# Half words turned by DMAs, scores in four full banks, a new VectorE order, and copies of the state's diagonal blocks

## The chip, the cores and the metric

One core of a Trainium2 chip runs the whole program in one launch. The metric is the device time in microseconds (us), the median over several runs. TensorE (PE) multiplies matrices, VectorE (DVE), ScalarE (ACT) and GpSimd (POOL) do the rest, SyncE (SP) issues most DMAs.

## The reference

A transformer block on x of shape (2, 2048, 512), float32:

```python
xn  = layernorm(x)                       # no affine part
# linear attention with decay, 16 heads of 32, chunks of 128 tokens
h   = rmsnorm(xn, qkv_norm_w);  q, k, v = h @ ternary(qkv_w).T
scores = einsum('bhtd,bhsd,hts->bhts', q, k, mask)        # within a chunk
o   = scale * (scores @ v + (q * lam_t) @ S)              # S: state, 32 x 32 per head
S   = lam_T * S + (k * lam_rev).T @ v
att = rmsnorm(rmsnorm(o, norm_w), proj_norm_w) @ ternary(proj_w).T
# feed-forward: 8 routed experts (top 2), width 256, and a shared expert, width 1024
router = softmax(xn @ w_gate)
ffn = sum over the two chosen e of c_e * (silu(xn @ g_e) * (xn @ u_e)) @ d_e  +  shared(xn)
out = x + att + ffn
```

## The kernel before

Products that need more than float16 are done with two half words: a high one, the float16 of a value, and a low one, the float16 of what is left. A product of two split values takes three passes of float16 matmuls (high by high, high by low, low by high); the ternary weights are exact in float16, so q, k, v and the projection take two passes.

The program runs in blocks, with all engines meeting between them: the setup of the weights; `attention` (16 steps); `shared(0)`, the shared expert on the first half of the tokens, beside which VectorE and ScalarE route the tokens and split the experts' weights; `routed()`, 72 tiles of 128 gathered rows; and `shared(1)`, the shared expert on the second half and the final sums.

A step of `attention` takes one chunk of 128 tokens of both sequences (u = 0 and 1). It is software-pipelined: in step n each engine works on the back part of chunk n (scores, outputs, state, norms, projection) and on the front part of chunk n+1 (its q, k, v, router logits), and VectorE already norms chunk n+2. The order of the work is written out by hand, per engine, in the functions `step` of `attention`; each engine goes through its list in order and waits on semaphores. PSUM has a ring of three banks (class `Ring`, which lists what passes through them in which order), a tensor `sc` of four banks for the scores and one bank `o_ps`.

What the change touches in a step:

- `xn_turn` (L624): TensorE transposes the normed tokens of the next chunk, ScalarE copies them out (`take_xnT`, L807), makes the high half words of h (`h_high`, L822, with the norm weight as scale) and of xn (`x_high`, L814); VectorE makes the low ones of h (`h_low`, L972), GpSimd those of xn (`x_low`, L1160).
- `scores` (L671): for each u four sets of four heads, each into two banks of `sc`, of which a set uses half; VectorE scales and masks each set (`decayed_scores`, L1026). The sets of u = 0 of the next chunk stand around v0 in TensorE's list.
- `o_back` (L709) transposes the output of a u back to token order; `o_square`, `o_mean`, `normed` (L853, L1052, L1065) are the first RMS norm, `on_squares`, `second_norm` (L863, L1073 to L1077) the second; GpSimd multiplies by the weight (`weighted`, L1183); TensorE transposes (`o_turn`, L727), ScalarE and VectorE split (`y_high`, L869, `y_low`, L1083), TensorE projects (`proj`, L736), VectorE adds the residual (L1093).
- `outer` makes k^T v for all pairs of heads of a group, `masked_kv` (L1043, VectorE) keeps the diagonal blocks by a multiplication with a 0/1 mask, and GpSimd updates the state (`update`, L1175, L1178); `decayed_q` (L1166) is GpSimd's too.
- VectorE also norms chunk n+2: `row_stats` (L923), `norm_stats` (L930 to L940), `norm` (L945, L949), `norm_factors` (L956 to L964), and takes the maxima of a part of the experts' weights (`weight_maxima`, L988).

xn goes to `xn_dram` in float32 for the gather of the routed tiles, its half words to `xT_dram` for the shared expert. In `routed()` a tile is gathered (L1250, GpSimd), split (L1918, ScalarE; L1850, GpSimd), turned by a DMA transpose that SP issues (L1823), and multiplied (L1280, L1287).

Of the kernel before, what the change touches and what calls it, by code (L numbers as in the profile page):

```python
# [12 lines left out]
P = 128  # L13
# [44 lines left out]
class Ring:  # L58
# [4 lines left out]
    FRONT = ["xnT0", "xnT1", "q0", "q1", "rt", "k0", "k1", "v0", "v1"]  # L63
    STEP = ["xnT0", "xnT1", "kTr0", "ot0", "kv0", "q0", "q1", "kTr1", "ot1", "rt", "onT0", "k0", "kv1", "k1", "proj0",
            "onT1", "v0", "v1", None, None, "proj1"]
    LAST = ["kTr0", "ot0", "kv0", "kTr1", "ot1", "onT0", "kv1", "proj0", "onT1", "proj1"]
# [38 lines left out]
def build(nc, x, qkv_w, qkv_nw, proj_w, proj_nw, norm_w, s, w_gate, w_gu, w_dn, w_sgu, w_sdn, out):  # L105
# [7 lines left out]
    xn_dram = nc.dram_tensor("xn_dram", [B * N, C], F32, kind="Internal").ap()  # L113
    xT_dram = nc.dram_tensor("xT_dram", [NCH, P, KT, 2, B * P], F16, kind="Internal").ap()
# [4 lines left out]
    xn_steps = xn_dram.rearrange("(b n p) c -> n p b c", b=B, p=P)  # L119
# [6 lines left out]
    with ExitStack() as kept:  # L126
# [40 lines left out]
        bmask = sb(attn, "bmask", [P, P])  # L167
        nw_b = sb(attn, "nw_b", [P, DIM])
        pnw_b = sb(attn, "pnw_b", [P, DIM])
        hw = sb(attn, "hw", [P, KT])  # L170
# [13 lines left out]
        with setup_ctx as c:  # L184
# [16 lines left out]
            qnw_c = sb(c, "qnw_c", [P, KT])  # L201
# [49 lines left out]
            SMALL = 16 * (1 + HPT + 5)  # L251

            @block.scalar
            def _(act):
                with nc.allow_non_contiguous_dma(reason="small vectors laid out as columns"):
# [7 lines left out]
                    act.dma_start(qnw_c[:], qkv_nw.rearrange("(k p) -> p k", p=P)).then_inc(in_small, 16)  # L263
# [48 lines left out]
            def _(v):  # L312
# [8 lines left out]
                link(v.memset(bmask[:], 0.0))  # L321
                for h in range(HPT):
                    v.memset(bmask[HD * h:HD * h + HD, HD * h:HD * h + HD], 1.0)
# [49 lines left out]
                v.tensor_scalar(hw[:], qnw_c[:], scales[:, 0:1], 1.0 / X_SCALE, ALU.mult, ALU.mult)  # L373
# [43 lines left out]
def mask_heads():  # L417

    return [HPT * (2 * (s // 2) + gg) + 2 * (s % 2) + jj for s in range(4) for jj in range(2) for gg in range(2)]


def attention(nc, ctx, sb, sem, k):
# [3 lines left out]
    qkvT, projT, wg16, ginv, mask, lamq, lamrev, lamT, bmask = (k[x] for x in "qkvT projT wg16 ginv mask lamq lamrev lamT bmask".split())  # L426
    nw_b, pnw_b, hw, alpha, state = (k[x] for x in "nw_b pnw_b hw alpha state".split())
    ident16, ounit, ounit2, xl, xl_in = (k[x] for x in "ident16 ounit ounit2 xl xl_in".split())
    x_steps, x1_steps, xn_steps, NCH, B = k["x_steps"], k["x1_steps"], k["xn_steps"], k["NCH"], k["B"]
# [10 lines left out]
    with ExitStack() as c:  # L440
# [3 lines left out]
        xnT = sb(c, "xnT", [P, KT, T2])  # L444
        x16 = sb(c, "x16", [P, 2, KT, 2, T2], F16)
        wraw = sb(c, "wraw", [P, 2, START[4]])
        hh = sb(c, "hh", [P, KT, T2], F16)
        hl = sb(c, "hl", [P, KT, T2], F16)
# [4 lines left out]
        probs = sb(c, "probs", [P, B, 4, 4, P])  # L453
# [5 lines left out]
        yh = sb(c, "yh", [P, B, KT, P], F16)  # L459
        yl = sb(c, "yl", [P, B, KT, P], F16)  # L460
# [34 lines left out]
        xn_out = [sem(c, f"xn_out{i}") for i in range(2)]  # L495
        x1_out = [sem(c, f"x1_out{i}") for i in range(2)]
        xT_out = [sem(c, f"xT_out{i}") for i in range(2)]
        wraw_in = [sem(c, f"wraw_in{i}") for i in range(2)]
        names = ("xhigh_ready xlow_ready wmax_ready stats_ready stats_seen mv_ready ve_ready sd_ready rstd_ready xn_ready rve_ready hv_ready hv2_ready hsd_ready "
                 "r_ready r2_ready kscale_ready xnT_ready hh_ready h_ready q_ready k_ready v_ready qlam_ready "  # L500
                 "o_full logits_ready kvm_ready kS_ready ss1_ready z1_ready sq1_ready g1a_ready "
# [22 lines left out]
        def after(q, par):  # L524
            return (q, 1) if par == 0 else (q + 1, 0)

        READ = {"xnT": "xnT_ready", "rt": "logits_ready", "q": "q_ready", "k": "k_ready", "v": "v_ready",
                "kTr": "kS_ready", "kv": "kvm_ready", "ot": "oT_ready", "onT": "yl_ready", "proj": "x1_ready"}
# [23 lines left out]
        def _(sp):  # L552
# [10 lines left out]
            def store_xn(q, par):  # L563
                n = 2 * q + par
                sp.wait_ge(S["xn_ready"], 2 * n + 2)
                sp.dma_start(xn_steps[n] if isinstance(n, int) else xn_steps[bass.ds(n, 1)][0], xn[:, par]
                             ).then_inc(xn_out[par], 16)
# [6 lines left out]
            def store_xT(q, par):  # L574
                n = 2 * q + par
                sp.wait_ge(S["xlow_ready"], n + 1)
                sp.dma_start(xT_dram[n] if isinstance(n, int) else xT_dram[bass.ds(n, 1)][0], x16[:, par]
                             ).then_inc(xT_out[par], 16)

            def prologue():  # L580
                for done_sem in k["setup_sems"]:
                    sp.sem_clear(done_sem)
                store_xn(0, 0)
                load_weights(0, 0)
                store_xT(0, 0)

            def step(q, par, front, norm):
                n = 2 * q + par
                if norm:
                    sp.wait_ge(S["xn_ready"], 2 * n + 2)  # L590
                    load_xl(q + 1, par)
# [3 lines left out]
                sp.wait_ge(S["x1_ready"], 2 * n)  # L595
                load_xr(q, par)
                if front:
                    store_xn(*after(q, par))
                    sp.wait_ge(S["wmax_ready"], n)
                    load_weights(*after(q, par))  # L600
                for u in range(B):
                    if u == 1 and front:
                        store_xT(*after(q, par))
                    sp.wait_ge(S["x1_ready"], 2 * n + u + 1)
                    dst = x1_steps[n] if isinstance(n, int) else x1_steps[bass.ds(n, 1)][0]
                    sp.dma_start(dst[:, u], x1[:, u]).then_inc(x1_out[u], 16)

            run_steps(sp, prologue, step)
            for par in range(2):
# [1393 lines left out]
```

## Time and profile before

| | us |
|---|---|
| median of 3 runs (1401.72 to 1403.88) | 1403.2 |
| the profiled execution's own time | 1401.92 |
| its span, first to last instruction | 1400.2 |
| TensorE busy | 1281.1 |
| VectorE busy | 695.2 |
| GpSimd busy | 527.0 |
| ScalarE busy | 514.0 |

Mean granted TensorE clock: 0.973. An engine's busy time counts from an instruction's start to its end, so pipelined matmuls overlap: two neighbours that take 0.27 us each can start 0.11 us apart. In a timeline the first number is the start, the second the time to the end of the group in that row.

### The profile page before, as it was taken

Reading aid. Unit: us, or ns where it says so; the run is one execution under the profiler, and the core shown is the slowest. Engines: PE = TensorE matmul, PEld = TensorE weight load, DVE = VectorE, ACT = ScalarE, POOL = GpSimd, SP = SyncE. Lnnn points to the kernel's source line nnn. Section 1 sums busy time; section 2 is a strip of 40 time slices with the busy share of each in tenths; the row PEclk is TensorE's granted clock in tenths of the full one; section 3 lists DMA queues with packets and bytes.
Section 4 is the critical chain, followed back from the end, with each engine's and each line's share of the span. In section 5 each row is a group of like instructions: output and inputs, shape, how many; then the busy total and the mean of one; then the engine's idle time right before and its main releaser. Section 6 shows DMA issues by size and latency. Waiting matters only on the chain. (4 is left out here: it accounts for less than half of the span.)

```text
span 1400.2 us, 29499 instructions
## 1 busy us (share of the span) xinstructions
PE 1281.1 (91%) x10418; PEld 879.9 (63%) x10418; DVE 695.2 (50%) x1606; ACT 514.0 (37%) x1034; POOL 527.0 (38%) x467
## 2 busy tenths in 40 slices
PE   1499999999999994999999969999999969999997
PEld 1477777667776673777777734444444447777775
DVE  4477877878878766883333322222222213333323
ACT  3444444444444434432323224544445411111111
POOL 0333344333444332024541035555554542444333
PEclk9699999999999997999999989999999989999999
DMA  5213443334433334524552358888888861443333
GB/s 173 95 60 129 154 145 109 109 131 142 161 109 109 131 125 162 180 93 105 107 138 102 33 136 183 188 194 190 186 191 186 192 190 65 179 164 135 135 136 121
DMA packets 174072, 195.06 MB, mean 139 GB/s; under 512 B 100976, under 2 KB 107248, under 8 KB 174000
## 3 DMA queue, kind: packets, MB, share of 16 engines
q1 hardware_dynamic: 158464, 156.17, 38.0%
q0 software_dynamic: 13328, 37.04, 10.0%
q8 instruction: 55, 0.90, 0.3%
q10 hardware_dynamic: 2208, 0.82, 0.2%
q14 instruction: 17, 0.14, 0.0%
HBM read 117.55 MB, written 56.77 MB: 124 GB/s over the span
## 5 line engine op out<-in xcount | busy, mean ns | idle before, releaser
L1269 PE MATMUL gu<-xT,WG 128*128 128x256 f16 x3072 | 350.3, 275 | 23.5 <-DMA x1s<-x_dram 11.8
L1269 PEld LDWEIGHTS gu<-xT,WG 128*128 128x128 f16 x3072 | 302.7, 99 | 74.8 <-DVE WD L1556 12.4
L1280 PE MATMUL rgu<-WG,raw 128*128 x876 | 215.1, 382 | 14.4 <-issue 10.9
L1695 DVE SCALAR_TENSOR_TENSOR actv<-gu,up_inv,sg 128x512 f32<-128x512 f32 x64 | 48.0, 751 | 252.8 <-ACT sg L1532 252.6
L1532 ACT ACTIVATE sg<-gu,gate_inv 128x512 f32<-128x512 f32 x64 | 43.9, 686 | 319.2 <-PE gu L1269 319.2
L1287 PE MATMUL yp<-WD,ah 128*128 128x512 f16 x512 | 152.3, 379 | 1.0 <-DVE al L1700 1.0
L1280 PEld LDWEIGHTS rgu<-WG,raw 128*128 128x128 f16 x876 | 86.1, 98 | 105.5 <-issue 23.2
L1850 POOL TENSOR_TENSOR xsp<-xg,xsp 128x512 f16<-128x512 f32 x75 | 86.7, 1157 | 105.2 <-ACT xsp L1918 105.2
L655 PE MATMUL ring<-hh,qkvT 128*128 128x256 f16 x512 | 116.4, 276 | 6.0 <-DVE hl L972 6.0
L1250 POOL DMA_INDIRECT xg<-xn_dram,idx x77 | 73.8, 958 | 123.9 <-POOL xsp L1850 66.4
L655 PE MATMUL ring<-hl,qkvT 128*128 128x256 f16 x512 | 116.4, 275 | 0.0
L1765 POOL DMA_INDIRECT raw<-y_dram,gidx x64 | 63.6, 994 | 133.7 <-DVE ys L1676 105.4
L1970 DVE TENSOR_TENSOR alr<-rat,ahr 128x256 f16<-128x256 f32 x72 | 30.5, 424 | 160.0 <-ACT ahr L1938 160.0
L1160 POOL TENSOR_TENSOR x<-xnT,x 128x1024 f16<-128x1024 f32 x16 | 34.3, 2142 | 198.8 <-ACT x L814 198.8
L1749 POOL DMA_INDIRECT slot_dram<-payload,posi x64 | 62.8, 981 | 116.5 <-DVE posi L1645 57.8
L1287 PE MATMUL yp<-WD,al 128*128 128x512 f16 x256 | 97.0, 379 | 0.0
L1026 DVE SCALAR_TENSOR_TENSOR probs<-sc,r,mask 128x512 f32<-128x512 f32 x128 | 89.7, 742 | 3.4 <-PE sc L671 3.4
L1287 PE MATMUL ryp<-WD,ahr 128*128 x288 | 85.9, 379 | 0.0
L1287 PEld LDWEIGHTS yp<-WD,ah 128*128 128x128 f16 x512 | 49.7, 98 | 49.3 <-DVE al L1700 2.5
L1924 ACT ACTIVATE raw<-ryp,out_inv 128x512 f32<-128x512 f32 x72 | 49.5, 687 | 65.9 <-PE ryp L1287 65.9
L1183 POOL TENSOR_TENSOR on<-on,pnw_b 128x512 f32<-128x512 f32 x32 | 40.7, 1273 | 77.1 <-DVE on L1065 77.1
L1700 DVE TENSOR_TENSOR al<-actv,ah 128x512 f16<-128x512 f32 x64 | 46.5, 726 | 44.5 <-ACT ah L1535 44.5
(237 smaller groups left out, 2163.2 us busy)
## 6 DMA issues: line engine op xcount, KB each, us to landing
y_dram<-raw SPq DMA_DIRECT2D x72, 256.0 KB
xl<-in_L_attn_x SPq DMA_DIRECT2D x16, 512.0 KB, 4.5
xn_dram<-xn SPq DMA_DIRECT2D x16, 512.0 KB, 6.4
wraw<-in_L_ffn_w_gate_up SPq DMA_DIRECT2D x16, 512.0 KB, 6.9
xT_dram<-x SPq DMA_DIRECT2D x16, 512.0 KB, 2.8
xr<-in_L_attn_x SPq DMA_DIRECT2D x16, 512.0 KB, 5.9
x_dram<-x SPq DMA_DIRECT2D x32, 256.0 KB, 2.1
xT<-xT_dram SPq DMA_DIRECT2D x16, 512.0 KB, 6.9
```

The costliest lines, as they stand in the source:

```text
L655: ins = pe.matmul(bank[:, g * T2:(g + 1) * T2], qkvT[:, kk, a:a + P], h[:, kk, :], start=(kk == 0 and h is hh), stop=(kk == KT - 1 and h i ...
L1026: v.scalar_tensor_tensor(out=probs[:, u, s].rearrange("p (j g) t -> p j (g t)", j=2), in0=sc[:, 2 * pair:2 * pair + 2, 0:2 * P], scalar=r[ ...
L1250: pool.indirect_dma_start(out=xg[:, par], out_offset=None, in_=xn_dram, in_offset=bass.IndirectOffsetOnAxis(ap=idx[:, par, 0:1], axis=0)). ...
L1269: ins = pe.matmul(gu[:, h, f * tokens:(f + 1) * tokens], w[:, kk, b, a0:a0 + P], x[:, kk, a], start=(kk == 0 and (a, b) == PASSES[0]), sto ...
L1280: ins = pe.matmul(gu[bank][:], x(kk, a), w[:, 0, kk, b, :], start=(i == 0), stop=(i == len(done) - 1))
L1287: ins = pe.matmul(y[:], act_hl[a][:, f, :], w[:, f, b, :] if len(w.shape) == 4 else w[:, 0, f, b, :], start=(first and f == 0 and (a, b) = ...
L1695: v.scalar_tensor_tensor(out=actv[:, g % 2], in0=gu[g % 2][:, 1].rearrange("p (f t) -> p f t", f=FT), scalar=up_inv[:, 1:2], in1=sg[:], op ...
L1700: v.tensor_tensor(al[:, g % 2], actv[:, g % 2], ah[:, g % 2], ALU.subtract).then_inc(S["al_ready"], 1)
L1749: pool.indirect_dma_start(out=slot_dram, out_offset=bass.IndirectOffsetOnAxis(ap=posi[:, kk, t:t + 1], axis=0), in_=payload[:, kk, t, :], ...
L1765: pool.indirect_dma_start(out=gy[:, u, i], out_offset=None, in_=y_dram, in_offset=bass.IndirectOffsetOnAxis(ap=gidx[:, u, i:i + 1], axis=0 ...
L1850: pool.tensor_tensor(xsp[:, par, 1], xg[:, par], xsp[:, par, 0], ALU.subtract).then_inc(S["low_ready"], 1)
L1924: act.activation(ysb[:, par], yp[par][:], ACT.Copy, scale=out_inv[:, 0:1]).then_inc(S["y_ready"], 1)
```

## The change

All transposes of half words become DMA transposes. h and xn are split in token order (`hs`, `xs`), and so is the second norm's output (`ys`); SP turns each [128, 1024] float16 tile into [128, 8, 128]. GpSimd multiplies xn by the norm weight (`weighted_h`). The half words of xn in token order go to `xs_dram`, from where the routed tiles are gathered already split, four tiles deep, so `routed()` has no split any more. The scores of a u fill all four banks and are masked in two operations of 1024 columns. The diagonal blocks are copied by ScalarE, four small copies a u, into a tile that was set to zero once. VectorE's, ScalarE's, GpSimd's and SP's lists are reordered.

```diff
-    STEP = ["xnT0", "xnT1", "kTr0", "ot0", "kv0", "q0", "q1", "kTr1", "ot1", "rt", "onT0", "k0", "kv1", "k1", "proj0",
-            "onT1", "v0", "v1", None, None, "proj1"]
+    STEP = ["kTr0", "ot0", "kv0", "q0", "q1", "kTr1", "ot1", "rt", "k0", "kv1", "k1", "proj0", "v0", "v1", "proj1"]
...
# SP
+            def turn_h(q, par):
+                n = 2 * q + par
+                if not (isinstance(n, int) and n == 0):
+                    wait_apart(sp, S["v_ready"], 2 * n, S["sp_passed"])
+                for u in range(B):
+                    wait_apart(sp, S["hl_ready"], 2 * n + u + 1, S["sp_passed"])
+                    sp.dma_start_transpose(hT[:, u], hs[:, u].rearrange("p a c -> p (a c)")).then_inc(hT_in[u], 16)
...
             def step(q, par, front, norm):
                 n = 2 * q + par
+                if front:
+                    turn_h(*after(q, par))
+                    turn_x(*after(q, par))
...
                 if front:
-                    store_xn(*after(q, par))
                     sp.wait_ge(S["wmax_ready"], n)
                     load_weights(*after(q, par))
+                    store_xs(*after(q, par))
+                    store_xT(*after(q, par))
                 for u in range(B):
+                    turn_y(u, q, par)
+                store_x1(0, q, par)
...
# TensorE
             def step(q, par, front, norm):
-                if front:
-                    xn_turn(0, *nxt, st)
-                    xn_turn(1, *nxt, st)
                 k_turn(0, q, par, st)
-                scores(1, q, par, (0, 1))
+                scores(1, q, par)
                 outputs(0, q, par, st)
-                scores(1, q, par, (2, 3))
...
-                o_turn(0, q, par, st)
...
                 proj(0, q, par, st)
                 if front:
-                    scores(0, *nxt, (0, 1))
-                o_turn(1, q, par, st)
-                if front:
+                    scores(0, *nxt)
                     project("v0", *nxt, st)
-                    scores(0, *nxt, (2, 3))
                     project("v1", *nxt, st)
                 proj(1, q, par, st)
...
# ScalarE
+            def take_kv(u, q, par, st):
...
+                for j in range(HPT):
+                    own = slice(HD * j, HD * j + HD)
+                    ins = act.activation(kvm[own, u, :, own], bank[own].rearrange("p (g e) -> p g e", g=KT)[:, :, own],
+                                         ACT.Copy)
...
                 take_oT(1, q, par, st)
                 o_square(1, q, par)
-                y_high(0, q, par, st)
+                o_root(1, q, par)
+                if norm:
+                    norm_roots(q + 1, par)
                 if front:
                     take("k0", *nxt, st)
-                o_root(1, q, par)
+                on_squares(1, q, par)
+                y_high(1, q, par)
                 if front:
                     take("k1", *nxt, st)
-                on_squares(1, q, par)
+                take_kv(1, q, par, st)
...
# VectorE, the whole new order
                 scaled_k(0, q, par, st)
+                decayed_scores(1, q, par)
                 o_mean(0, q, par)
                 normed(0, q, par)
+                weight_maxima(q, par, (1, 2, 3))
+                scaled_k(1, q, par, st)
+                second_norm(0, q, par)
+                y_low(0, q, par)
                 if has_norm:
                     row_stats(0, q + 1, par)
                     row_stats(1, q + 1, par)
                 if front:
                     take_logits(*nxt, st)
+                if has_norm:
+                    norm_stats(q + 1, par)
                 o_mean(1, q, par)
                 normed(1, q, par)
                 if has_norm:
+                    norm(q + 1, par)
+                    norm_factors(q + 1, par)
                 second_norm(1, q, par)
+                y_low(1, q, par)
                 weight_maxima(q, par, (0,))
+                residual(0, q, par, st)
+                if front:
+                    decayed_scores(0, *nxt)
+                else:
+                    weight_scales()
+                if has_norm:
+                    h_low(q + 1, par)
                 residual(1, q, par, st)
...
# GpSimd
+            def weighted_h(q, par):
+                n = 2 * q + par
+                for u in range(B):
+                    pool.wait_ge(S["xn_ready"], 2 * n + u + 1)
+                    if not (isinstance(n, int) and n == 0):
+                        pool.wait_ge(S["hl_ready"], 2 * n + u - 1)
+                    pool.tensor_tensor(hn[:, u], xn[:, par, u], hw_b[:], ALU.mult).then_inc(S["hn_ready"], 1)
...
                 weighted(1, q, par)
+                if norm:
+                    weighted_h(q + 1, par)
                 update(1, q, par)
...
# experts
-                            ins = pe.matmul(gu[:, h, f * tokens:(f + 1) * tokens],
+                            ins = pe.matmul(gu[:, h, f * tokens:(f + 1) * tokens].rearrange("p (u t) -> p u t", u=B),
                                             w[:, kk, b, a0:a0 + P],
-                                            x[:, kk, a], start=(kk == 0 and (a, b) == PASSES[0]),
+                                            x[:, :, a * KT + kk, :], start=(kk == 0 and (a, b) == PASSES[0]),
...
                 def _(pool):
-                    def low_part(q, par):
...
+                    for r in range(XG, TURNS):
+                        pool.wait_ge(turned[r % XH], 16 * ((r - XG) // XH + 1))
+                        gather(pool, r)
```

## Rows read from the trace of the kernel before

**Rows 1.** Windows, whole attention and one microsecond: length, busy per engine, granted clock, DMA share, GB/s.

```profile
61.00:541.00 480.00, 454.47 (x4978) 343.27 (x4979) 372.67 (x891) 207.52 (x487) 183.01 (x128) 0.99 0.37 127
...
531.00:532.00 1.00, 1.00 (x6) 1.00 (x7) 0.47 (x1) 0.03 (x1) 0.92 (x2) 0.50 1.05 382
```

**Rows 2.** Timeline of TensorE, one step: start, us, engine, line, what, [idle before].

```profile
297.60 0.66 PE L709 MATMUL o_ps<-ident,oT 128*128 128x128 f32 x4
...
304.74 0.74 PE L671 MATMUL sc<-qT,kT 32*128 32x128 f32 x16
305.41 0.66 PE L727 MATMUL ring<-ident,on 128*128 128x128 f32 x4
...
312.14 0.38 PE L736 MATMUL ring<-projT,yh 128*128 128x512 f16 x1 [0.87 <-ACT vS L832]
...
313.87 1.04 PE L624 MATMUL ring<-ident,xn 128*128 128x128 f32 x8
314.88 0.66 PE L679 MATMUL ring<-ident,kT 128*128 128x128 f32 x4
...
327.05 0.66 PE L709 MATMUL o_ps<-ident,oT 128*128 128x128 f32 x4
```

**Rows 3.** Timelines of VectorE and of GpSimd, where both work at once.

```profile
302.52 1.18 DVE L934 TENSOR_SCALAR ve<-mv 128x2 f32<-128x2 f32 x1
...
302.42 1.27 POOL L1183 TENSOR_TENSOR on<-on,pnw_b 128x512 f32<-128x512 f32 x1 [1.68 <-DVE on L1065]
...
57.89 0.48 DVE L972 SCALAR_TENSOR_TENSOR hl<-xnT,hw,hh 128x256 f16<-128x256 f32 x1 [3.55 <-ACT hh L822]
...
59.09 2.34 DVE L972 SCALAR_TENSOR_TENSOR hl<-xnT,hw,hh 128x256 f16<-128x256 f32 x1
...
58.88 2.26 POOL L1160 TENSOR_TENSOR x<-xnT,x 128x1024 f16<-128x1024 f32 x1 [9.35 <-ACT x L814]
...
329.56 0.20 DVE L1052 TENSOR_SCALAR z<-ss,r2m 128x1 f32<-128x1 f32 x1
...
327.87 2.35 POOL L1166 TENSOR_TENSOR qlam<-qT,lamq 128x1024 f32<-128x1024 f32 x1
```

**Rows 4.** Timeline of VectorE, the operations whose place changes.

```profile
309.35 1.00 DVE L949 TENSOR_SCALAR xn<-xl,mv,rstd 128x512 f32<-128x512 f32 x2
...
314.74 0.15 DVE L956 RECIPROCAL r<-hsd 128x2 f32<-128x2 f32 x1
...
315.66 0.69 DVE L1034 TENSOR_TENSOR kS<-ring,kscale 128x512 f32<-128x512 f32 x1
...
322.59 0.20 DVE L1052 TENSOR_SCALAR z<-ss,r2m 128x1 f32<-128x1 f32 x1
...
323.46 0.75 DVE L1065 SCALAR_TENSOR_TENSOR on<-o_ps,g,nw_b 128x512 f32<-128x512 f32 x1
324.12 1.28 DVE L923 BATCH_NORM_STATS2 stats<-xl 128x6 f32<-128x512 f32 x2
...
328.95 0.69 DVE L1083 TENSOR_TENSOR yl<-ring,yh 128x512 f16<-128x512 f32 x1 [1.54 <-ACT yh L869]
```

**Rows 5.** Timeline of ScalarE, one copy out of PSUM.

```profile
303.12 0.60 ACT L842 ACTIVATE kT<-ring 128x512 f32<-128x512 f32 x1 [1.95 <-PE ring L655]
```

**Rows 6.** DMA queues and issues, 90 to 520 us, then 820 to 1125 us.

```profile
q1 hardware_dynamic: 25552, 53.49, 36.2%
...
q1 hardware_dynamic: 86307, 37.24, 54.6%
...
raw<-xsp SPq DMA_TRANSPOSE x73, 3.1
```

**Rows 7.** Timelines of SP and TensorE where routed() starts, and of TensorE late in attention.

```profile
816.58 1.36 SPq L1823 DMA_TRANSPOSE raw<-xsp  x1
...
822.16 6.48 PE L1280 MATMUL rgu<-WG,raw 128*128 x18 [10.89 <-issue]
...
530.82 0.90 PE L709 MATMUL o_ps<-ident,oT 128*128 128x128 f32 x3 [2.99 <-ACT oT L847]
```

More of the change, by code:

```diff
@@ L646, in project @@
                     for kk in range(KT):
-                        for h in (hh, hl):
-                            ins = pe.matmul(bank[:], h[:, kk, i * P:(i + 1) * P], qkvT[:, kk, 2 * DIM:3 * DIM],
-                                            start=(kk == 0 and h is hh), stop=(kk == KT - 1 and h is hl))
+                        for a in range(2):
+                            ins = pe.matmul(bank[:], hT[:, i, a * KT + kk, :], qkvT[:, kk, 2 * DIM:3 * DIM],
+                                            start=(kk == 0 and a == 0), stop=(kk == KT - 1 and a == 1))
@@ L720, in outer @@
                 ins.then_inc(done, 1)
[L722 to L728 removed]
             def proj(u, q, par, st):
                 n = 2 * q + par
[L732 removed]
+                pe.wait_ge(yT_in[u], 16 * (n + 1))
                 bank, done = fill(pe, f"proj{u}", st)
                 for g in range(KT):
[L735 to L737 removed]
+                    for a in range(2):
+                        ins = pe.matmul(bank[:], yT[:, u, a * KT + g, :], projT[:, g, :],
+                                        start=(g == 0 and a == 0), stop=(g == KT - 1 and a == 1))
                 ins.then_inc(done, 1)
             def prologue():
[L741 to L742 removed]
                 for name in ("q0", "q1"):
@@ L946, in norm @@
                 v.wait_ge(S["rstd_ready"], n + 1)
-                v.wait_ge(xn_out[par], 16 * q)
+                if not (isinstance(n, int) and n < 2):
+                    v.wait_ge(S["xlow_ready"], 2 * n - 2)
                 for u in range(B):
@@ L1133, in step @@
                 if has_norm:
-                    norm_stats(q + 1, par)
-                masked_kv(1, q, par, st)
+                    norm(q + 1, par)
+                    norm_factors(q + 1, par)
                 second_norm(1, q, par)
+                y_low(1, q, par)
                 weight_maxima(q, par, (0,))
+                residual(0, q, par, st)
                 if front:
-                    decayed_scores(0, *nxt, (0, 1))
-                residual(0, q, par, st)
-                if has_norm:
-                    norm(q + 1, par)
-                y_low(1, q, par, st)
-                if front:
-                    decayed_scores(0, *nxt, (2, 3))
+                    decayed_scores(0, *nxt)
                 else:
                     weight_scales()
+                if has_norm:
+                    h_low(q + 1, par)
                 residual(1, q, par, st)
-                if has_norm:
-                    norm_factors(q + 1, par)
             run_steps(v, prologue, step)
@@ L1713, in step @@
                                  unit_experts)[i]()
-                            if half == 0 and last and g == 1:
-                                v.wait_ge(slot_in, 16)
-                                index(v, 0, 0)
-                                index(v, 0, 1)
                         if last:
@@ L1799, in routed @@
                 block = c.enter_context(nc.Block())
-                def later(q, par, tiles):
-                    return q + (par + tiles) // 2, (par + tiles) % 2
                 def run_steps(eng, step):
@@ L1855, in _ @@
-                    for r in range(3):
-                        low_part(r // 2, r % 2)
-                    def step(q, par, first):
-                        low_part(*later(q, par, 3))
-                    run_steps(pool, step)
-                    pool.wait_ge(xg_in[0], 16 * (SLOT_TILES // 2 + 3))
-                    pool.wait_ge(xg_in[1], 16 * (SLOT_TILES // 2 + 2))
+                    for r in range(XG, TURNS):
+                        pool.wait_ge(turned[r % XH], 16 * ((r - XG) // XH + 1))
+                        gather(pool, r)
@@ L1904, in some @@
                         for i in range(UNROLL):
-                            tile(UNROLL // 2 * h + i // 2, i, first and i == 0, places)
+                            tile(h, i, first and i == 0, places)
                     some(0, True)
```

395 lines of the change are left out of this document (166 added, 229 removed).

## The prediction

> **What bounds the kernel now.** The page comes first: TensorE is busy for 1281 of the span's 1400 us, and its line in the 40 slices is at 9 nearly everywhere. The windows say the same of the 16 steps of attention: 454 of 480 us, clock 0.99, VectorE 373, DMA 0.37 [rows 1]. The routed tiles are TensorE-bound too. So the stage to read is attention, and the view is the timeline of one step. From one o_back(1) to the next it is 327.05 - 297.60 = 29.45 us [rows 2]. TensorE stands still in it only for about 2 us: 0.87 before proj1, the rest around the split scores and in semaphores. The last step has no front part, so 15 such periods count.
>
> **What leaves TensorE.** Eight transposes of xn (313.87 to 314.88, 1.0 us) and two times four of the second norm (305.41 starts one) at half that, 0.5 each: 2.0 us. The wait before proj1 (0.87) goes, since the onT bank and the ring's two blanks go. If nothing else became late, a period would be 29.45 - 2.0 - 0.9 = 26.6 us, and 15 of them 43 us less. The question is which chain then ends last.
>
> **The chain that I see: from o_back(1) to the scores of the next chunk.** Let x be the start of o_back(1). TensorE has this to do until scores(0): before 304.74 - 297.60 = 7.1 us, without o_turn 6.6. But scores(0) needs k1 copied out, and ScalarE now copies k1 after on_squares(1) and y_high(1), thus after the root of VectorE's second_norm(1); before, k1 stood ahead of on_squares(1). And VectorE now puts norm and norm_factors of chunk n+2 between normed(1) and second_norm(1). Step by step:
> - z(1), the mean of the first norm: before at x + 2.5 (329.56), just behind y_low(0) at 328.95. y_low(0) comes 2.7 us earlier, having lost its transposes and copy (my estimate from GpSimd's product and one copy of 0.60, [rows 3, 5]). Between the two now stand row_stats (1.28, [rows 4]), the logits (0.2) and norm_stats, some 0.6 of small operations and the 1.18 of `ve` [rows 3]: 3.2 us. z(1) is at x + 3.0.
> - from z to the end of `on`: 322.59 to 323.46 + 0.75, 1.62 us [rows 4]. Call the end T = x + 4.6.
> - T starts on3(1) on GpSimd (1.27 us), and right behind it come the two new weighted_h, of the same form as on3 (1.27 each).
>
> Here a behaviour of the rows decides. Where VectorE and GpSimd work at once, VectorE's operations on SBUF alone stand still: `ve`, two elements, took 1.18 us beside GpSimd's product of 302.42 and ended with it; an hl of 57.89 took 0.48 alone, that of 59.09 took 2.34 beside GpSimd's x_low of 58.88. That last pair also shows the order: GpSimd got in between two operations of VectorE that followed each other without a gap. An operation on one element did not stand still (z at 329.56, 0.20, beside decayed_q) [rows 3]. The operations of norm and norm_factors (xn; r2, rv, rc, r2m, kscale) are of the kind that did, and before they all ran while GpSimd was idle. Now:
> - xn waits for on3(1), to T + 1.35; its two operations take 1.0 [rows 4]: T + 2.35.
> - weighted_h of u = 0 takes 1.27: r2 waits to T + 3.6 and ends at 3.8.
> - weighted_h of u = 1 gets in, 1.27: T + 5.05. The rest of the factors, about 0.7 of the 0.92 from 314.74 to 315.66 [rows 4]: T + 5.75.
> - z2 0.2, root 0.2, y_high 0.5 and k1's copy 0.6 (a copy: [rows 5]), 0.1 to TensorE: T + 7.4 = x + 12.0.
>
> So TensorE, done at x + 6.6, stands still for 5.4 us in this stretch. From scores(0) to the next o_back(1) it has work: two times 0.67 for the scores (304.74 to 305.41), v0, v1 and proj1 at 1.73 each (eight matmuls of 512 columns, 312.14 to 313.87), and from k_turn 314.88 to 327.05 12.2 us, where nothing changes [rows 2]: 1.3 + 5.2 + 12.2 = 18.7. The period is 12.0 + 18.7 = 30.7 us, 1.25 more than before, and 15 of them +19 us.
>
> Of xn the trace has no row beside a busy GpSimd. For it speaks its speed: 512 columns in 0.5 us, where bn_stats on as many takes 0.64 (half of 1.28) [rows 4]. The Trainium skill (SBUF — State Buffer, "Who interferes with whom") says that copies, casts and tensor_scalar can enter modes that need the port pair shared with GpSimd, so that one of the two engines stands still for a whole instruction. By that xn is held, as summed here; were only operations with two SBUF operands held, xn would be free and the stretch shorter by 1.1 us a step.
>
> **What else changes, and what hides it.**
> - VectorE: four masks of 512 columns for a u become two of 1024, about 0.6 us less in a step, and masked_kv's two 0.69 go. Neither lies in the stretch above. Zero; had they counted, at most 2 us a step.
> - ScalarE: eight small block copies, bounds 0.15 and 0.6 each (a one-column operation and a full copy [rows 5]), beside TensorE's work; I take 0.3. The copies for v0 and the kv banks come later than k1's but before their banks are asked for.
> - Turned h: SP issues two turns once v1 is copied; issue 1.36 [rows 7], landing 3.1 [rows 6], so hT is there 5 us after v1; q0 starts over 7 us after it. Hidden, with 2 us to spare. SP's loads and stores of a step stand behind these turns, and turn_y behind all of them.
> - Turned y0: y_low(0) ends near x, the turn lands at x + 3.2 on an empty queue and proj0 is due at x + 4.9. Loads, xs and xT are still being moved then, up to 3 us: TensorE may wait 1.4 us before proj0. In my sum that lies within the 5.4 us; without them it would show. Turned y1 is issued about 1 us before scores(0); proj1 comes 4.8 us after it: hidden.
> - DMA work: 53.49 MB took 36.2% of 430 us, 0.76 us for 256 KB. In the routed stretch 54.6% of 305 us, less 73 stores at 0.76, over 73 turns gives 1.5 us a turn, twice a copy of that size [rows 6]. A step goes from 10.7 (0.362 x 29.45) to 19.8 us: under the period.
>
> The Trainium skill (Advanced Engine Details and Errata, "X-Bar Transpose (TRN2)") has transposing DMAs as fast as plain ones; the rows say twice the time. By the page a step would hold 15.3 us of DMA work instead of 19.8; the sum is the same by both.
> - Shared expert: its matmuls (and q's, k's) read the moving operand as two pieces of 128 columns instead of 256 in a row. No row shows such a read. Bounds: 0, and 10% of the 0.11 us between two such matmuls, some 45 us over 4096 of them. I take 0: the routed stage's and the projection's matmuls of 512 columns and these of 256 all run at one pace a column.
> - routed(): bound by TensorE, so the split that goes gives nothing a tile. At its start the first turn was issued at 816.58, behind the split, and TensorE began at 822.16 [rows 7]; now the rows are there already: -1 to -3, I take -2.
> - Ends of attention: proj1 of the last step gets 2 us later, under the scales' chain (weight_scales), which stays ahead of the last residual. Zero, bounds -1 and +3.
>
> **Sum.** 1401.9 (the profiled execution's own time) + 19 - 2 = 1419; the runs' median is 1.3 above it: 1420.
>
> **Rivals.**
> - The port is no matter for these operations (faster). Then T to k1 is xn 1.1, factors 0.9, z2, root, y_high, k1 and 0.1: 3.8 us; scores(0) at x + 8.4, the period 27.1, 15 x -2.35 = -35: 1366. For it: no row has xn held. Against: `ve` and hl.
> - VectorE keeps the port once it has it, so weighted_h of u = 1 doesn't get in: 1.27 less a step, 29.4: about 1400. The pair at 59 us speaks against.
> - The clock falls too (slower still). Late in attention TensorE stood still for 2.99 us before 530.82, three transposes then took 0.90, and the window 531 to 532 was granted 0.50 [rows 1, 7], the level of 1.2 GHz. My sum has a gap of up to 5.4 us in each step, perhaps cut in two by proj0. Three microseconds at half pace cost 1.5: a period of 32.2, +41 - 2, 1442. For it the two gaps near 3 us that the trace has, both with that end; against, that TensorE is busy over 80% around the gap, which it was not there.
> - Turns slower than 1.5 us when four stand in one queue, or the two-piece reads cost: +15 to +45, over 1430. This decides from 2 us a turn (22.7 us of DMA work and all of turn_y behind it).
> - The change does what it says and nothing is late: 1360.
>
> **Chances.** Forecast 0.36; the clock with it 0.20; VectorE keeps the port 0.12; no matter of ports, or nothing late, 0.24; turns or reads 0.08. Range 1362 to 1443; the forecast's own is 1406 to 1432. Within 0.2% (2.8 us) is what a measurement can't tell from no change: 0.08. Faster 0.36, slower 0.56.
>
> **What would show it.** After: xn (L949's successor) near 1.7 us in its first operation, one of r2, rv near 1.4 in each step; ScalarE's root of z2(1) with the longest wait, on VectorE; scores(0) waiting for k1's copy by 3 to 5 us; period 30.7. Wrong if xn keeps its 0.54 us in all steps (27.1), or if TensorE's longest wait is for DMAs (yT, hT). A granted clock under 0.95 in attention is the third rival. The routed tiles should keep 4.1 us, and the shared expert its matmuls' 0.11.

## The result, and the profile after

The changed kernel takes 1438.4 us in the median of 4 runs (1431.9 to 1444.1), the kernel before 1402.5 beside it: a ratio of 1.0255, 95% interval 1.0203 to 1.0307. It is slower by 36 us. The forecast was 1420, slower by 18; the time lies at the rival in which the clock falls too, 1442. The profiled execution took 1441.9 us, with a span of 1440.1 us and a mean granted clock of 0.951 (before: span 1400.2, 0.973).

Windows of the changed kernel over attention and over single microseconds of one step (length, busy time per engine with instructions, granted clock, DMA share, GB/s):

```profile
60.00:590.00 530.00, 460.34 (x4736) 340.31 (x4736) 373.45 (x758) 215.96 (x568) 231.72 (x173) 0.91 0.62 165
...
299.00:300.00 1.00, 1.00 (x14) 1.00 (x17) 1.00 (x1) 0.95 (x4) 0.21 (x1) 0.53 0.00 0
304.00:305.00 1.00, 1.00 (x3) 0.30 (x2) 0.43 (x1) 0.00 (x0) 0.00 (x0) 0.50 0.00 0
306.00:307.00 1.00, 1.00 (x7) 0.41 (x6) 0.00 (x0) 0.07 (x1) 0.00 (x0) 1.00 0.00 0
332.00:333.00 1.00, 0.84 (x18) 0.87 (x22) 1.00 (x2) 0.96 (x5) 0.00 (x0) 1.00 0.00 0
333.00:334.00 1.00, 1.00 (x22) 1.00 (x17) 1.00 (x2) 0.97 (x3) 0.87 (x1) 0.59 0.42 84
336.00:337.00 1.00, 1.00 (x5) 0.44 (x4) 1.00 (x3) 0.00 (x0) 0.00 (x0) 0.70 0.00 0
```

Against [rows 1], TensorE is busy for 87% of the stretch instead of 95%, and the mean granted clock is 0.91 instead of 0.99. The single windows say how: in each step the clock drops to 0.50, the 1.2 GHz level, for a stretch, and comes back. In one step the stretch runs from 299 to about 306 us, in the next from 333 to 337, and so on in turn: 6.8 and 3.4 us, if twice what each window lacks of 1.00 is added up.

TensorE's timeline of that step (start, us, line, what, idle time before and its releaser):

```profile
298.82 2.92 PE L695 MATMUL sc<-qT,kT 32*128 32x128 f32 x32 [2.16 <-issue]
...
321.35 0.66 PE L731 MATMUL o_ps<-ident,oT 128*128 128x128 f32 x4
...
327.94 1.90 PE L750 MATMUL ring<-projT,yT 128*128 128x512 f16 x8 [1.55 <-DMA yT<-ys]
332.16 2.25 PE L695 MATMUL sc<-qT,kT 32*128 32x128 f32 x32 [2.32 <-issue]
```

o_back(1) starts at 321.35 and scores(0) at 332.16, 10.8 us later, where TensorE has 6.9 us of work (6.6 forecast). It stands still twice: 1.55 us before proj0, for the turn of y(0), and 2.32 us before scores(0). In [rows 2] the step's largest gap is 0.87. Behind the wait it works at half pace: the 32 matmuls of the scores take 2.92 and 2.25 us, where they take 1.72 at full clock.

The two engines that the prediction's chain runs through, VectorE first, then ScalarE and GpSimd:

```profile
324.23 0.20 DVE L1050 TENSOR_SCALAR z<-ss,r2m 128x1 f32<-128x1 f32 x1
...
325.15 0.75 DVE L1063 SCALAR_TENSOR_TENSOR on<-o_ps,g,nw_b 128x512 f32<-128x512 f32 x1
...
326.10 1.89 DVE L957 TENSOR_SCALAR xn<-xl,mv,rstd 128x512 f32<-128x512 f32 x2
327.91 0.15 DVE L964 RECIPROCAL r<-hsd 128x2 f32<-128x2 f32 x1
328.10 1.03 DVE L966 TENSOR_TENSOR r<-r 128x2 f32<-128x2 f32 x1
329.05 0.16 DVE L967 TENSOR_SCALAR rv<-r 128x2 f32<-128x2 f32 x1
329.12 1.24 DVE L968 TENSOR_SCALAR rc<-r,ounit 128x2 f32<-128x2 f32 x1
...
330.68 0.14 DVE L1071 TENSOR_SCALAR z<-ss 128x1 f32<-128x1 f32 x1
```

```profile
330.86 0.20 ACT L872 ACTIVATE sq<-z 128x1 f32<-128x1 f32 x1 [4.20 <-DVE z L1071]
330.96 0.61 ACT L878 ACTIVATE ys<-on 128x512 f16<-128x512 f32 x1
331.48 0.58 ACT L838 ACTIVATE kT<-ring 128x512 f32<-128x512 f32 x1
...
325.98 1.26 POOL L1183 TENSOR_TENSOR on<-on,pnw_b 128x512 f32<-128x512 f32 x1 [2.28 <-DVE on L1063]
...
327.69 2.65 POOL L1161 TENSOR_TENSOR raw<-xn,hw_b 128x512 f32<-128x512 f32 x2 [0.44 <-DVE xn L957]
```

T, the end of `on`, is 325.9. xn's pair takes 1.89 us beside on3(1), which ends at 327.24; in [rows 4] it takes 1.00. r2 and rc, two elements in each partition, take 1.03 and 1.24 us beside the two products of weighted_h. ScalarE, having nothing that it may do, waits 4.20 us for z2(1), and k1's copy, which scores(0) wait for, ends at 332.06. So the chain is the one forecast, step by step.

Where the 39.9 us between the two spans are, by the starts of `on`: up to the first one -2.0; 15 periods 484.26 us instead of 440.26, +44.0; the last step +0.1; all behind attention -2.2. A period is 32.28 us in the mean, in turn about 33.3 and 31.7.

### The profile page after: what moved, and what is told of

The parts are those of the page before. It is cut to its first block and busy times, and to the rows that moved or that the text cites. A ratio compares the mean times of both kernels' runs of the same rounds, so it can differ in the third digit from the quotient of the medians.

```text
span 1440.1 us, 27983 instructions
## 1 busy us (share of the span) xinstructions
PE 1282.9 (89%) x10162; PEld 875.7 (61%) x10162; DVE 693.5 (48%) x1396; ACT 482.6 (34%) x1039; POOL 486.5 (34%) x437
## 5 line engine op out<-in xcount | busy, mean ns | idle before, releaser
L1248 POOL DMA_INDIRECT raw<-xs_dram,slots x73 | 69.4, 951 | 299.6 <-DMA raw<-raw 241.3
L680 PE MATMUL ring<-hT,qkvT 128*128 128x256 f16 x1024 | 122.3, 276 | 19.8 <-DMA hT<-hs 18.4
L680 PEld LDWEIGHTS ring<-hT,qkvT 128*128 128x128 f16 x1024 | 101.3, 99 | 32.7 <-issue 20.2
L695 PE MATMUL sc<-qT,kT 32*128 32x128 f32 x1024 | 68.1, 327 | 28.9 <-issue 28.9
L750 PE MATMUL ring<-projT,yT 128*128 128x512 f16 x256 | 67.3, 411 | 29.0 <-DMA yT<-ys 29.0
L695 PEld LDWEIGHTS sc<-qT,kT 32*128 32x128 f32 x1024 | 61.0, 224 | 39.8 <-issue 39.8
L1031 DVE SCALAR_TENSOR_TENSOR probs<-sc,r,mask 128x1024 f32<-128x1024 f32 x64 | 79.1, 1278 | 11.7 <-PE sc L695 11.7
L673 PE MATMUL ring<-qkvT,hT 128*128 128x512 f16 x256 | 76.0, 463 | 0.0
```

Of the source, the lines that this page charges most:

```text
L673: ins = pe.matmul(bank[:], hT[:, i, a * KT + kk, :], qkvT[:, kk, 2 * DIM:3 * DIM], start=(kk == 0 and a == 0), stop=(kk == KT - 1 and a == 1))
L680: ins = pe.matmul(bank[:, g * T2:(g + 1) * T2].rearrange("p (u t) -> p u t", u=B), qkvT[:, kk, w0:w0 + P], hT[:, :, a * KT + kk, :], start ...
L695: ins = pe.matmul(sc[:, j, g * P:(g + 1) * P], kT[rows, par, g, u * P:(u + 1) * P], qT[rows, par, g, u * P:(u + 1) * P], start=True, stop= ...
L750: ins = pe.matmul(bank[:], yT[:, u, a * KT + g, :], projT[:, g, :], start=(g == 0 and a == 0), stop=(g == KT - 1 and a == 1))
L1031: v.scalar_tensor_tensor(out=probs[:, u, pair].rearrange("p j g t -> p j (g t)"), in0=sc[:, 2 * pair:2 * pair + 2], scalar=r[:, par, u:u + 1],
L1248: pool.indirect_dma_start(out=xg[:, r % XG], out_offset=None, in_=xs_dram, in_offset=bass.IndirectOffsetOnAxis(ap=slots[:, r, 0:1], axis=0 ...
```

## The experiments

All times are medians in us; the ratio is to the kernel before, run in the same job (1401.5, 1402.4 and 1399.2). All edits are to the changed kernel. "Steady" is said of the steps from about the fifth on.

**Unneeded matmuls in both gaps.** TensorE gets something to do ahead of the waits for k1 and for y(0), which stay as they are; only the waits for free banks come ahead of the added matmuls, which write there.

```diff
+                    for pair in range(2):
+                        pe.wait_ge(sc_free[pair], 2 * n + u)
+                    for i in range(9):
+                        pe.matmul(sc[:, i % 4, :], hT[:, 0, 0, :], qkvT[:, 0, 0:DIM], start=True, stop=True)
...
+                bank, done = fill(pe, f"proj{u}", st)
+                if u == 0:
+                    for _ in range(6):
+                        pe.matmul(bank[:], hT[:, 0, 0, :], qkvT[:, 0, 0:DIM], start=True, stop=True)
                 pe.wait_ge(yT_in[u], 16 * (n + 1))
-                bank, done = fill(pe, f"proj{u}", st)
```

> TensorE gets work that nobody needs while it would stand still: 6 matmuls of 512 columns ahead of the wait for y0, 9 ahead of the wait for k1 (1.3 and 1.9 us at full pace, against gaps of 1.6 and 2.2 us). Theory (the clock falls over the gaps, on top of the waits): granted clock in attention 0.98 instead of 0.91, period 30.0 to 30.9 us instead of 32.3, total 1438 - 15 x 1.8 = 1411, 1403 to 1420. Rival (the chain through VectorE sets the period, the half pace is absorbed by later waits): no change, 1433 to 1443. Rival (more TensorE work only costs): slower, 1450.

1408.8 (1407.7 to 1411.7), ratio 1.0050 [1.0033, 1.0066]; mean clock 0.979. More work makes it 30 us faster. ScalarE's wait for z2(1) is what it was (61.7 us in 28 times, the longest 4.2, in the changed kernel), so the chain is untouched. The window over attention shows the clock, and TensorE's timeline what changed (waits: engine, line, for whom, sum, times, longest):

```profile
ACT sq L879 <- DVE z L1078: 62.3, 30, 4.2
```

```profile
90.00:540.00 450.00, 435.30 (x4611) 319.46 (x4612) 350.20 (x710) 199.18 (x525) 216.22 (x161) 1.00 0.67 183
```

```profile
314.49 1.89 PE L757 MATMUL ring<-projT,yT 128*128 128x512 f16 x8
316.22 2.11 PE L691 MATMUL sc<-qkvT,hT 128*128 128x512 f16 x9
319.15 1.72 PE L699 MATMUL sc<-qT,kT 32*128 32x128 f32 x32 [0.83 <-issue]
```

The steady period is 30.1 us each time, with no stretch at half pace. So a period's 33.3 and 31.7 split: 30.1 is the late chain, 3.2 and 1.6 the clock, about half of the 6.8 and 3.4 us. By the medians some 29 of the 36 us are the clock's (1438.4 less 1408.8), though the fillers may cost a little themselves. In the two traced executions, 30.1 us apart, 26.4 of them lie before the last `on` of attention. What stands behind it, with the same code in both, takes 863.1 and 859.3 us; in the ten traces of the changed kernel and its variants it takes 852 to 866, so a few us between two totals need not come from attention.

**GpSimd forms h's product last.** weighted_h goes behind update(1), so VectorE's factors meet a quiet GpSimd.

```diff
-                if norm:
-                    weighted_h(q + 1, par)
                 update(1, q, par)
+                if norm:
+                    weighted_h(q + 1, par)
```

> GpSimd does its two products by h's norm weight after update(1) instead of before it. Theory (they hold VectorE's factors, so the root of z2 and k1's copy are late): r2 and rc take 0.16 and 0.22 again, xn stays at 1.9 for two, k1 is out 1.9 us earlier, the gap before scores(0) goes from 2.2 to under 0.5, the clock stays up, period 28.7 to 29.8, total 1385 to 1402. Rival (waits for the turned y0, DMA): that gap stays at 1.6 and the period at 31 or more, over 1420.

1397.4 (1388.4 to 1404.4, 10 runs), ratio 0.9978 [0.9954, 1.0002]. The factors that were held are free, and only they: xn stays beside on3(1).

```profile
307.72 1.89 DVE L957 TENSOR_SCALAR xn<-xl,mv,rstd 128x512 f32<-128x512 f32 x2
...
309.71 0.16 DVE L966 TENSOR_TENSOR r<-r 128x2 f32<-128x2 f32 x1
...
309.86 0.22 DVE L968 TENSOR_SCALAR rc<-r,ounit 128x2 f32<-128x2 f32 x1
```

r2 falls from 1.03 to 0.16 us, rc from 1.24 to 0.22, ScalarE's longest wait for z2(1) from 4.2 to 2.3. A steady period is 28.65 us, with four of 29.9 to 31.7 among them, behind gaps before proj0 of 2.1 to 2.9 us after which the clock still falls. That the ten runs spread over 16 us for this reason is my reading; one execution is traced. Nor did the gap before the scores go under 0.5 us everywhere, as expected: in four steps it is 1.0 to 1.2.

**ScalarE takes k1 ahead of the second root.** VectorE and GpSimd stay as they are, held operations included; only k1's copy no longer stands behind them.

```diff
                 on_squares(1, q, par)
                 y_high(1, q, par)
                 if front:
                     take("k1", *nxt, st)
+                on_root(1, q, par)
```

`on_root` is the wait for z2 and the root, taken out of `on_squares`.

> ScalarE copies k1 before it waits for the second root of u = 1; nothing else moves. VectorE is held by GpSimd as before. Theory (it is k1's place behind that wait that turns VectorE's lateness into TensorE's): scores(0) waits no more, xn and r2 are as slow as now, the clock stays up, y1's turn may be just late for proj1; period 28.6 to 30, total 1385 to 1405. Rival (VectorE is late for other readers too, so the gap only moves): period 31 to 32, total 1420 to 1435.

1394.0 (1390.9 to 1401.2), ratio 0.9955 [0.9934, 0.9975]. rc still takes 1.24 us, and it does no harm:

```profile
308.95 1.90 PE L750 MATMUL ring<-projT,yT 128*128 128x512 f16 x8 [1.32 <-DMA yT<-ys]
310.78 1.72 PE L695 MATMUL sc<-qT,kT 32*128 32x128 f32 x32
...
313.49 3.61 PE L673 MATMUL ring<-qkvT,hT 128*128 128x512 f16 x16 [0.99 <-ACT kvm L853]
```

The scores follow proj0 at once, the period is 28.51 us in ten steps of the fifteen, and in those the clock is 1.00 throughout, with gaps before proj0 of up to 1.86 us. The first four have gaps of 3.0 to 3.9 us there, and periods of 31 to 34. So nearly all of what VectorE's slowness cost came through one queue entry, a copy that stood behind a root. A little of it stays: the copies of the diagonal blocks of u = 1 still stand behind that root, and TensorE waits 0.5 to 1.5 us for them before v0 in each steady step (0.99 in the one shown).

**No product at all.**

> Leaves out the product of xn with h's norm weight, so GpSimd has 2.5 us less in a step and h is split from xn itself. Theory (the products on GpSimd hold VectorE): r2 and rc fast, xn still held by on3 (1.9 for two), period 28 to 29.5, total 1380 to 1397, within 8 us of the kernel with those products later. Rival (xn is slow of itself, or the loss is in the DMAs): over 1415.

1389.0 (1386.2 to 1391.0), ratio 0.9911 [0.9893, 0.9930], steady period 28.20, with two of 29.9. It leaves out the multiplication by the norm weight, so it is a bound and not a version. The product's whole presence costs 49 us, and the two reorderings above, which keep it, get 41 and 44 of them.

**VectorE's order changed back.** The next tile's norm and factors behind second_norm(1) and y_low(1).

```diff
+                second_norm(1, q, par)
+                y_low(1, q, par)
                 if has_norm:
                     norm(q + 1, par)
                     norm_factors(q + 1, par)
-                second_norm(1, q, par)
-                y_low(1, q, par)
```

> VectorE alone changed back to an order nearer the old one: the norm of the next tile and its factors come after the second norm and y_low of u = 1 instead of ahead of them. My theory: y(1) gets ready earlier, but h's product on GpSimd starts later by as much, and k1's copy on ScalarE still waits for the second root of u = 1, whose own wait is gone, so the wait for k1 shrinks by about 2 to 4 us in VectorE's terms but the tail behind it (h's turn for the next tile) comes later: period 30.5 to 32, total 1415 to 1437 us. Rival (the VectorE order is all there is to it): the scores' gap goes under 1 us, period under 29 us, total under 1400 us.

1419.7 (1418.0 to 1426.9), ratio 1.0132 [1.0091, 1.0173]; half of the loss is back. The scores' gap is gone altogether, but of ten steady periods four are 29.3 and six 30.7 to 31.3: the waits have moved.

```profile
316.83 1.90 PE L750 MATMUL ring<-projT,yT 128*128 128x512 f16 x8 [2.00 <-DMA yT<-ys]
318.66 1.72 PE L695 MATMUL sc<-qT,kT 32*128 32x128 f32 x32
...
324.66 1.89 PE L750 MATMUL ring<-projT,yT 128*128 128x512 f16 x8 [0.72 <-DVE x L1089]
...
333.14 2.12 PE L680 MATMUL ring<-hT,qkvT 128*128 128x256 f16 x18 [0.89 <-issue]
```

```profile
317.01 1.00 DVE L957 TENSOR_SCALAR xn<-xl,mv,rstd 128x512 f32<-128x512 f32 x2
...
318.12 1.03 DVE L966 TENSOR_TENSOR r<-r 128x2 f32<-128x2 f32 x1
```

The longest gap is now the one before proj0, for y(0)'s turn: 2.0 us here, and behind four of 2.3 to 2.6 us in the steady steps the clock falls. Besides, proj1 waits for VectorE's residual, and TensorE stands still ahead of q0's matmuls (L680), which read the turned h; the norm that h comes from starts 3.7 us behind the start of `on` (313.32), not 0.95. That h is what they wait for is my reading, the row says only "issue". Here no product is running when xn starts (the next one starts at 317.71, 0.3 us before xn's end), and the pair takes 1.00: with the 1.89 of the other kernels, its price beside GpSimd is measured both ways.

**Unneeded matmuls before the scores alone.** The gap before proj0 stays empty.

```diff
+                    for pair in range(2):
+                        pe.wait_ge(sc_free[pair], 2 * n + u)
+                    for i in range(9):
+                        pe.matmul(sc[:, i % 4, :], hT[:, 0, 0, :], qkvT[:, 0, 0:DIM], start=True, stop=True)
```

> As the changed kernel, with only the 9 unneeded matmuls ahead of the wait for k1's copy; the gap before the first projection (1.7 us, waiting for y(0)'s turn) stays empty. If the clock falls on account of the pair of gaps, or of the later one, which this change made, it stays up here: clock 0.975 to 0.98, period 30.0 to 30.6 us, total 1406 to 1418 us. Rival: the gap before the projection is enough to bring it down: clock 0.95 to 0.96, a period of 31.5 us or more, total 1427 us or more.

1417.9 (1407.6 to 1421.3, 8 runs), ratio 1.0098 [1.0072, 1.0123]; clock 0.975. From the fifth step on the period is 30.1, at full clock, though TensorE still stands still for up to 1.5 us before proj0; the first four take 30.7 to 33.4. So in the steady part a gap of that size before proj0 does not bring the clock down by itself; the one before the scores, which this change made, has to be there. Of the 9 us to the kernel with both gaps filled, attention holds 2 in the traced executions, up to its last `on`; the rest lies behind it.

**Both reorderings** (GpSimd's product last, and k1 ahead of the root).

> Both reorderings at once: GpSimd forms h's product after its last state update, and ScalarE takes k1 before the second root of u = 1. My theory: each alone already empties the wait ahead of the first scores (0.8 to 1.7 us are left of it), and both take away the same wait, so they hardly add: a period of 28.2 to 28.6 us as with k1 early alone, no stretch at half pace in the steady part, total 1386 to 1397 us. Rival: they add, because two different things held the scores (product on GpSimd, root on ScalarE): a period of 28.0 us or less and a total under 1385 us.

1394.1 (1391.5 to 1401.8), ratio 0.9931 [0.9908, 0.9955]: they don't add, as expected. But the clock did not stay up, as I had said that it would (the traced execution is the slowest of the five, 1401.8): periods of 27.7 to 27.9 alternate with 29.7 to 30.5, since the faster step now waits longer for y(0)'s turn, and the clock falls behind some of these waits (3.35 us for eight matmuls that take 1.90 at full pace).

```profile
256.88 3.35 PE L750 MATMUL ring<-projT,yT 128*128 128x512 f16 x8 [1.94 <-DMA yT<-ys]
...
285.89 1.90 PE L750 MATMUL ring<-projT,yT 128*128 128x512 f16 x8 [1.23 <-DMA yT<-ys]
```

**Both, and the weight loads behind y(0)'s turn.**

```diff
                 if front:
-                    sp.wait_ge(S["wmax_ready"], n)
-                    load_weights(*after(q, par))
                     store_xs(*after(q, par))
                     store_xT(*after(q, par))
-                for u in range(B):
-                    turn_y(u, q, par)
+                turn_y(0, q, par)
+                if front:
+                    sp.wait_ge(S["wmax_ready"], n)
+                    load_weights(*after(q, par))
+                turn_y(1, q, par)
```

> Both reorderings, and on SyncE's queue the weight loads of the next tile moved from ahead of the turn of y(0) to between the turns of y(0) and y(1), so that y(0)'s turn does not share the DMA engines with 1.3 MB of loads. With the scores no longer late, the gap of 1.3 to 1.4 us before the first projection (it waits for y(0)'s turn) is the only one left. If the turn is held up by the loads' traffic, the gap shrinks: period 27.3 to 28.2 us, total 1370 to 1384 us. Rival: the turn's 3 us are its own latency and the loads do not matter: period 28.4 to 28.6, total 1386 to 1397 us, as e5_both.

1375.8 (1373.4 to 1377.6), ratio 0.9804 [0.9774, 0.9834]: faster than both kernels, by 62 us than the changed one. Its timeline of a step and DMA waits in attention:

```profile
318.83 0.66 PE L732 MATMUL o_ps<-ident,oT 128*128 128x128 f32 x4
...
323.71 1.89 PE L751 MATMUL ring<-projT,yT 128*128 128x512 f16 x8
325.99 1.72 PE L696 MATMUL sc<-qT,kT 32*128 32x128 f32 x32 [0.38 <-issue]
```

```profile
PE ring L751 <- DMA yT<-ys: 8.2, 6, 2.3
```

From o_back(1) to the scores it is 7.2 us, next to TensorE's own work, and the period is 27.71 to 27.73 us in ten steps. Read turn by turn, y(1)'s lands 3.1 us after its issue in nearly every step of all these kernels. y(0)'s, which the loads precede or follow in SyncE's queue, lands after 6.0 us in the median in the changed kernel, 6.7 with both reorderings, and 4.2 here: the loads' traffic had held it up. TensorE's wait for turned y in attention is 24.5 us in the changed kernel, 34.1 with both reorderings, and 8.2 here.

**The loads' place alone.**

> The SyncE part of e6_three alone: the changed kernel with the weight loads of the next tile moved from ahead of the turn of y(0) to between the turns of y(0) and y(1), and nothing else. My theory: the first scores wait for k1's copy, 10.8 us after o_back(1), whatever the first projection does, so an earlier y(0) only moves idle time of TensorE from ahead of the projection to ahead of the scores: the gap ahead of the projection falls from 1.7 to under 0.8 us, that ahead of the scores grows from 2.2 to 3 us or more, the clock still falls, period 31.5 to 32.5 us, total 1428 to 1444 us: nothing of the 18 us that the same edit gave on top of the other two. Rival: it takes its gap away here too, and with the pair of gaps gone the clock stays up: period 31 us or less, clock 0.97 or more, total under 1420 us.

1433.3 (1428.0 to 1437.2), ratio 1.0249 [1.0227, 1.0271], against 1.0255 of the changed kernel: nothing clear of the noise, where the same edit gave 18 us on top of the other two.

```profile
ACT sq L873 <- DVE z L1072: 61.5, 27, 4.2
...
PE ring L751 <- DMA yT<-ys: 2.8, 2, 1.9
```

```profile
262.02 3.10 PE L696 MATMUL sc<-qT,kT 32*128 32x128 f32 x32 [4.05 <-issue]
...
326.95 3.11 PE L696 MATMUL sc<-qT,kT 32*128 32x128 f32 x32 [4.05 <-issue]
```

The wait for y is gone and the one before the scores is longer by it, 4.05 us in one piece. The clock falls after it as it did after the pair, and the periods are 33.2 and 31.7 again.

## Why the prediction was wrong in size

**The chain (right).** Forecast and measured, from o_back(1) at x: `on` ends x + 4.6, measured 4.55. xn ends T + 2.35, measured 2.1; the first factors after GpSimd's first product T + 3.8, measured 3.2; all factors T + 5.75, measured 4.9 (330.76); k1's copy read by the scores T + 7.4, measured 6.3. The small steps were each priced too high: scores(0) at x + 10.8, not 12.0. From scores(0) to the next o_back(1) TensorE needs 19.3 us at full clock (319.15 to 338.43 with matmuls in the gaps), not 18.7: the first scores take 1.72 and not 1.34, k_turn to o_back 12.4 and not 12.2. Together 30.1, where the forecast had 30.7.

**GpSimd gets in (right).** That weighted_h of u = 1 follows that of u = 0 with only rv (0.16 us) of VectorE getting in between (2.65 us for the two), and that xn is held, was the choice that set the sign. The terms of the rival "no matter of ports" add up to 3.6 us and not 3.8 (its total would be 1363), which changes nothing here. It and "VectorE keeps it" fall: r2 and rc take 0.16 and 0.22 us when GpSimd is quiet, 1.03 and 1.24 beside it, and the total moves by 41 us with them. The rule of the Trainium skill (SBUF — State Buffer, "Who interferes with whom"), by which xn, a tensor_scalar, is held as well, holds in the trace: its pair takes 1.00 us beside nothing and 1.89 beside on3(1).

**The clock (the step that failed).** The forecast let TensorE start at full pace after its gap, and gave the falling clock, as a rival, a chance of 0.20 at 1442. The argument against it was that TensorE is busy over 80% around the gap, which it was not where the trace of before showed 0.50. That was worth nothing: the clock fell in every step, after gaps such as 1.55 and 2.32 us, and in another kernel after a single 4.05. Filling both gaps gives 30 us back with the waits unchanged, so the forecast's own mechanism makes about 7 us of the 36 (1408.8 less the 1401.5 of before in that job), not 18, and the clock, which the sum had at nothing, the rest, some 29. The rival's size was "three microseconds at half pace cost 1.5", a period of 32.2; measured are 3.4 and 6.8 us in turn, costing 1.6 and 3.2, on a chain shorter by 0.6: 32.28. It came near through two errors that offset each other.

**Turned y0.** Forecast was a wait of up to 1.4 us before proj0, hidden within the chain: 1.0 to 1.7 measured in the steady steps, and hidden, as the loads' place alone shows. That it would be the next to show once the chain is mended was said, not what it costs: 18 us.

**What costs nothing.** The two-piece reads of the shared expert: 274 ns in the mean over 3072 matmuls, before 275.

```profile
L1267 PE MATMUL gu<-xT,WG 128*128 128x256 f16 x3072 | 349.3, 274 | 18.5 <-DMA x1s<-x_dram 13.7 <-PEq L1776 3.2 <-issue 1.4
L1278 PE MATMUL rgu<-WG,raw 128*128 x876 | 215.6, 383 | 15.2 <-issue 12.5 <-DMA raw<-raw 2.7
```

DMA work in a step: 0.62 of 32.28 us is 20.0, forecast 19.8, so a turn costs 1.5 us as taken from [rows 6]. No more turns are late than y(0)'s. The routed tiles keep their pace (383 ns, before 382).

**The start of routed() (wrong, small).** Forecast -2. TensorE's idle time before the first routed matmul is 11.64 us, against 10.89 in [rows 7]: no gain. The 2.2 us less behind attention lie elsewhere: 1.7 more up to the shared expert's first matmul, 3.7 less from the first routed matmul to the end. No experiment was made on either.

**The gain that was meant.** Forecast for "nothing late" was a period of 26.6 and 1360. The best version has 27.7 and 1375.8. TensorE still stands still in its steady step for 0.38 us before the scores and for 0.87 before k_turn(0) (two rows of ScalarE, one of TensorE):

```profile
331.51 0.63 ACT L820 ACTIVATE hs<-raw 128x512 f16<-128x512 f32 x1 [3.81 <-POOL raw L1167]
...
333.31 1.26 ACT L829 ACTIVATE vS<-ring,rv 128x512 f32<-128x512 f32 x2
...
334.05 0.66 PE L704 MATMUL ring<-ident,kT 128*128 128x128 f32 x4 [0.87 <-ACT vS L829]
```

The copy of v that k_turn(0) waits for stands in ScalarE's list behind the copies of h, and these wait for GpSimd's product, which is now GpSimd's last work of the step. Together 1.25 us, about what lies between 26.6 and 27.7; no run takes this wait away. The first four periods are long in most of the versions (28.7 to 35.3 us), with gaps before proj0 of 1.9 to 5.2 us for y(0)'s turn; with the loads moved on top of the two reorderings they are 28.1 to 29.6. Why the turns are later there than in the other steps stays open.

## What to carry to other kernels

Price a new wait of the busiest engine twice: its length, and a stretch at half clock behind it, when the trace has even one example of such a fall; TensorE was busy for 87% of attention here, and its clock fell in every step. Look in each in-order queue for a copy that TensorE waits for standing behind a small operation with a late input: moving that one copy took back 44 us here. And once a chain is cut, the transfer that hid beside it is the next to end last, so an edit that is worth nothing alone can be worth 18 us on top of the others.

## What was not expected of the hardware

- The stretches at half pace in attention lasted 3.4, 6.8 or 10.2 us, and their length did not follow that of the gap: after gaps of 4.05 us the granted clock fell in each step, for 6.8 and 3.4 us in turn. Single gaps before proj0 of 1.94 to 3 us had a fall behind them in some steps (1.94, 2.14, 2.30) and none in others (2.17, 2.22, and 2.93 in the kernel with matmuls before the scores); with VectorE's order changed back, two gaps of 2.29 us ended one with a fall and one without. Behind single ones of up to 1.9 us there was none, but in the kernel without the product two pairs of small ones, 0.65 and 1.34 us and 0.83 and 1.16, had a fall behind them, and pairs like them in other steps had none.
- GpSimd's two products in a row (2.65 us for the pair) let one operation of VectorE through between them: r2 is held to the end of the first and rv (0.16) passes, then rc is held to the end of the second. A reciprocal of two elements, started 0.2 us into the first product, is not held (327.91, 0.15 us).
- A transposing DMA of y lands 3.1 us after its issue with the loads out of its way; with 1.2 MB of loads issued some microseconds ahead of it, as for y(0) in the changed kernel, the median is 6.0 and the longest 8.5 us.
